# Graph kernel: tables and first projection in one stage, with keys and values projected under the tables

## The reference

```
q = (x @ Wq + bq).reshape(n, H, C)
k = (x @ Wk + bk).reshape(n, H, C)
v = (x @ Wv + bv).reshape(n, H, C)
e = (ea @ We).reshape(-1, H, C)
kj = k[src] + e
vj = v[src] + e
alpha = einsum('ehc,ehc->eh', q[dst], kj) / sqrt(C)
...
return out + x @ Ws + bs
```

## Time and profile before

| what | us |
|---|---|
| runs | 8291.74, 8230.95, 8294.77 |
| median | 8291.74 |
| profiled execution | 8250.71 |
| its span | 8248.9 |
| busy: PE, PEld, DVE | 3484.3, 2716.4, 3757.1 |
| busy: ACT, POOL | 2123.0, 3625.4 |

### The profile page before, as it was taken

How to read it: one execution, slowest core, us unless ns; L and a number is a source line. 1 busy time by engine, 2 the same in 40 slices (tenths; PEclk the granted TensorE clock), 3 DMA queues, 4 the chain that set the end, 5 groups by cost and what they waited for, 6 DMA issues and landing times. The chain is left out here.

```text
span 8248.9 us, 101168 instructions
## 1 busy us (share of the span) xinstructions
PE 3484.3 (42%) x20097; PEld 2716.4 (33%) x20099; DVE 3757.1 (46%) x8522; ACT 2123.0 (26%) x5629; POOL 3625.4 (44%) x3965
## 2 busy tenths in 40 slices
PE   3445544545444444444355457324233334333332
PEld 1344444444233334334232223112222223222322
DVE  5444444445644444444664347796233333223333
ACT  1333333333144434334322224255000001000001
POOL 1444443443154444443026650022666664566664
PEclk8676767677756656556666669656555566655556
DMA  3333333333332222222111111001111112111111
GB/s 115 118 104 104 109 108 103 109 107 101 106 92 83 81 84 81 81 80 75 48 51 32 32 36 58 18 0 67 43 44 44 44 45 77 57 44 45 45 44 49
DMA packets 371112, 569.20 MB, mean 69 GB/s; under 512 B 86858, under 2 KB 247772, under 8 KB 370524
## 3 DMA queue, kind: packets, MB, share of 16 engines
q0 software_dynamic: 140272, 311.94, 13.8%
q1 hardware_dynamic: 230764, 256.45, 9.4%
HBM read 509.24 MB, written 58.86 MB: 69 GB/s over the span
## 5 line engine op out<-in xcount | busy, mean ns | idle before, releaser
L682 POOL DMA_INDIRECT ring<-kv_table,idx x1568 | 1494.9, 953 | 1950.7 <-ACT pv L771 1268.1
L2017 POOL DMA_INDIRECT rows_in<-rel_table,idx x1568 | 1489.4, 950 | 808.3 <-issue 610.3
L1196 PE MATMUL ps_s<-rows_in,onehot 128*128 x3520 | 741.0, 393 | 1622.0 <-SPq L2033 850.6
L1196 PEld LDWEIGHTS ps_s<-rows_in,onehot 128*128 128x128 f32 x3520 | 683.0, 296 | 1680.0 <-issue 1679.0
L891 DVE TENSOR_TENSOR key<-ps_q,key 128x528 f32<-128x528 f32 x440 | 306.8, 707 | 1524.2 <-remote 1070.6
L1223 DVE TENSOR_TENSOR acc<-acc,ps_s 128x128 f32 x880 | 253.0, 288 | 1478.8 <-PE ps_s L1196 1065.2
L815 PE MATMUL ps_s<-pv,lent 128*128 128x136 f32 x3520 | 819.4, 386 | 106.6 <-DVE acc L874 94.9
L829 PE MATMUL ps_q<-qsplit,st 128*128 x5280 | 503.7, 255 | 739.9 <-DVE key L891 348.8
L815 PEld LDWEIGHTS ps_s<-pv,lent 128*128 128x128 f32 x3520 | 704.0, 279 | 145.7 <-DVE acc L874 118.1
L829 PEld LDWEIGHTS ps_q<-qsplit,st 128*128 128x128 bf16 x5280 | 413.3, 113 | 826.9 <-issue 801.3
L1726 PE MATMUL ps_f<-s_split,at_lo 128*128 128x392 bf16 x2112 | 510.6, 402 | 357.1 <-DVE found L1783 248.5
(11 more groups left out here) (322 smaller groups left out, 5058.1 us busy)
## 6 DMA issues: line engine op xcount, KB each, us to landing
dl_row<-dloc_slots SPq DMA_DIRECT2D x132, 640.0 KB
eb<-in_edge_attr SPq DMA_DIRECT2D x440, 128.0 KB
ring<-kv_table,idx POOLq DMA_INDIRECT x1568
rows_in<-rel_table,idx POOLq DMA_INDIRECT x1568
flags<-flag_rows SPq DMA_DIRECT2D x88, 168.0 KB
rel_table<-y_out SPq DMA_DIRECT2D x14, 1024.0 KB, 4.3
lo_row<-lo_rows SPq DMA_DIRECT2D x44, 256.0 KB
rel_table<-y_out SPq DMA_DIRECT2D x14, 768.0 KB, 3.6
```

Of the source, the lines that this page charges most:

```text
L682: pool.indirect_dma_start(ring3[:, s % (2 * RING), :], None, kv_table, bass.IndirectOffsetOnAxis(ap=idx[:, s:s + 1], axis=0))\
L1196: last_mm = pe.matmul(to, one(n, j), ring_rows(places[m], j), start=(j == 0), stop=(j == 1))
L2017: pool.indirect_dma_start(rows3[:, t, :], None, table, bass.IndirectOffsetOnAxis(ap=idx[:, t:t + 1], axis=0))\
```

## The change

`opening` takes the place of `tables` and of the first `conv_project`; there is one barrier less. The loads of x, weights and biases (ten) are issued behind the twelve of the tables.

Keys and values of all seven groups are made in a first loop. It begins when VectorE has copied the tile rows out of PSUM, for the loop uses that PSUM as its four places. ScalarE copies x to `xg` and the transposed x to `xt`, and takes the results out; PE multiplies a window with 256 columns and adds the bias by a second matmul of one row (`ones` by the bias row). SP stores them in a loop that stands ahead of the table stores on its queue. PE's loop stands ahead of the transposes of the extremes and of the three tables, ScalarE's ahead of its three copies.

Skips and queries are made in a second loop behind the turned tables: x is transposed a second time, GpSimd copies to `xg`, PE multiplies 256 columns per window, VectorE adds the biases, makes the parts in the same chain of seven, and ScalarE copies them to `qsplit`. SP stores the skips behind the table stores. The matmul that spreads the extremes (`ext_d`) stands behind PE's second loop, and VectorE's last operations on them behind its own.

```diff
-        def tables():
-            done = ExitStack()
+        def opening(x_in, qsplit):
...
+                ps_y = pb(done, "ps_y", [P, 2 * 1024])
+                ps_x = pb(done, "ps_x", [P, 1024])
                 ps_t = pb(done, "ps_t", [P, 512])
-                ps_e = pb(done, "ps_e", [P, 2 * 1024])
+                ps_row, ps_e = ps_y, ps_y
...
+                PLACES, N_LOADS, Q_LINKS = 4, 10, 7
+                kv3, sq3, qx3 = grouped(kv_out), grouped(sq_out), grouped(qx)
+                q3 = qsplit[:, :].rearrange("p (w k c) -> p w k c", k=3, c=QW)
+                place_in = lambda j: ps_y[:, j % PLACES * 512:j % PLACES * 512 + 2 * D]
...
+                        sp.dma_start(x_in[:, :], a["x"]).then_inc(project_in.sem, 16)
+                        for n, k in enumerate(("v", "k", "s", "q")):
+                            sp.dma_start(w_all[:, n * D:(n + 1) * D], a[f"L0_gnn_W{k}1"]).then_inc(project_in.sem, 16)
+                            sp.dma_start(b_all[:, n * D:(n + 1) * D],
+                                         a[f"L0_gnn_b{k}1"].partition_broadcast(P)).then_inc(project_in.sem, 16)
+                        sp.dma_start(we_b[:, :], a["L0_gnn_We1"][0, :].partition_broadcast(P)).then_inc(project_in.sem, 16)
+
+                        with sp.Fori(0, NG) as g:
+                            for (lo, hi), sig in zip(HALVES, kv_stored):
+                                sp.wait_ge(evacuated.sem, evacuated.at(g * G + hi))
+                                sp.sem_inc(issuing.sem, 1)
+                                sp.dma_start(kv_rows[:, bass.ds(g * G + lo, hi - lo), :], kv3[:, lo:hi, :]).then_inc(sig.sem, 16)
 
                         sp.wait_ge(chained.sem, LAYOUT_T)
...
                         sp.wait_ge(copied.sem, len(to_turn))
                         sp.dma_start(type_rows[0], et16_e[:, :]).then_inc(stored.sem, 16)
+
+                        with sp.Fori(0, NG) as g:
+                            for (lo, hi), sig in zip(HALVES, skip_stored):
+                                sp.wait_ge(added.sem, added.at(g * G + hi))
+                                sp.sem_inc(issuing.sem, 1)
+                                sp.dma_start(skip_of[:, bass.ds(g * G + lo, hi - lo), :], sq3[:, lo:hi, 0:D]).then_inc(sig.sem, 16)
                         sp.wait_ge(stored.sem, 16 * STORES)
+                        sp.dma_start(last_of, last_row[:, 0:SP // 2]).then_inc(last_in.sem, 16)
+                        for sig in kv_stored + skip_stored:
+                            sp.wait_ge(sig.sem, sig.at(16 * NG))
+                        sp.wait_ge(last_in.sem, 16)
...
                         dve.wait_ge(chained.sem, link.count[0])
+                        dve.sem_inc(of_rows.sem, 1)
...
+                        dve.wait_ge(project_in.sem, 16 * N_LOADS)
+                        with dve.Fori(0, NG) as g:
+                            for j in range(G):
+                                if j in starts:
+                                    sig = skip_stored[starts.index(j)]
+                                    dve.wait_ge(sig.sem, sig.at(g * 16))
+                                dve.wait_ge(made.sem, made.at(g * G + (NW + j + 1)))
+                                dve.tensor_tensor(sq3[:, j, :], place_in(j), b_all[:, 2 * D:4 * D], ALU.add).then_inc(added.sem, 1)
+                            dve.wait_ge(added.sem, added.at((g + 1) * G))
+                            dve.wait_ge(kept.sem, kept.at(g))
+                            q_link = chain(dve, q_chain, g * Q_LINKS)
+                            q_link(dve.tensor_scalar(qx3[:, :, 0:D], sq3[:, :, D:2 * D], float(C) ** -0.5, None, ALU.mult))
+                            q_link(dve.tensor_tensor(grouped(tmp), qx3[:, :, 0:D], we_b[:, :].unsqueeze(1).to_broadcast([P, G, D]), ALU.mult))
+                            q_link(dve.tensor_reduce(qx3[:, :, D:QW], tmp[:, :].rearrange("p (g h c) -> p g h c", g=G, h=H), AX.X, ALU.add))
+                            split3(dve, q_link, qx, rest, parts)
+                            assert q_link.count[0] == Q_LINKS
+                            dve.sem_inc(results.sem, 1)
...
+                        def half_of(g, first, biased):
+                            pe.wait_ge(got.sem, got.at(g + (1 if biased else NG + 1)))
+                            pe.wait_ge(xt_ready.sem, xt_ready.at(g + (0 if biased else NG)))
+                            for j in range(G):
+                                last_mm = pe.transpose(ps_x[:, j * D:(j + 1) * D], xg[:, j * D:(j + 1) * D], ident[:, :])
+                            last_mm.then_inc(x_turned.sem, 1)
+                            pe.wait_ge(xt_ready.sem, xt_ready.at(g + (1 if biased else NG + 1)))
+                            used_up = evacuated if biased else added
+                            for j in range(G):
+                                pe.wait_ge(used_up.sem, used_up.at(g * G + max(j - PLACES + 1, 0)))
+                                last_mm = pe.matmul(place_in(j), xt[:, j * D:(j + 1) * D], w_all[:, first:first + 2 * D],
+                                                    start=True, stop=not biased)
+                                if biased:
+                                    last_mm = pe.matmul(place_in(j), ones[0:1, 0:P], b_all[0:1, first:first + 2 * D],
+                                                        start=False, stop=True)
+                                last_mm.then_inc(made.sem, 1)
+
+                        pe.wait_ge(of_rows.sem, 1)
+                        pe.wait_ge(project_in.sem, 16 * N_LOADS)
+                        with pe.Fori(0, NG) as g:
+                            half_of(g, 0, True)
+
                         pe.wait_ge(chained.sem, LAYOUT_T)
                         pe.transpose(ps_t[0:2, 128:256], ext[:, :], ident[:, :]).then_inc(ext_s.sem, 1)
-                        pe.wait_ge(counted.sem, TC + 1)
-                        pe.matmul(ps_t[:, 256:258], ones[0:2, :], ext_d[:, :], start=True, stop=True).then_inc(ext_s.sem, 1)
+                        pe.wait_ge(evacuated.sem, evacuated.at(NW))
                         for n, (of, _) in enumerate(to_turn):
                             if n >= 2:
                                 pe.wait_ge(copied.sem, n - 1)
@@ -360,13 +457,56 @@
                                 last_mm = pe.transpose(ps_e[:, at:at + P], blocked(of)[:, b, :], ident[:, :])
                             last_mm.then_inc(turned.sem, 1)
 
+                        pe.wait_ge(copied.sem, len(to_turn))
+                        with pe.Fori(0, NG) as g:
+                            half_of(g, 2 * D, False)
+                        pe.wait_ge(counted.sem, TC + 1)
+                        pe.matmul(ps_t[:, 256:258], ones[0:2, :], ext_d[:, :], start=True, stop=True).then_inc(ext_s.sem, 1)
...
+                        def take(g, before):
+                            act_e.wait_ge(x_turned.sem, x_turned.at(g + (before // G + 1)))
+                            act_e.wait_ge(made.sem, made.at(g * G + before))
+                            act_e.copy(xt[:, :], ps_x[:, 0:G * D]).then_inc(xt_ready.sem, 1)
+
+                        def store_results(g):
+                            act_e.wait_ge(results.sem, results.at(g + 1))
+                            act_e.copy(q3[:, bass.ds(g * G, G), :, :],
+                                       parts[:, :].rearrange("p (k g c) -> p g k c", k=3, g=G)).then_inc(kept.sem, 1)
+
+                        def fetch_x(g):
+                            act_e.copy(xg[:, :], x_in[:, bass.ds(g * (G * D), G * D)]).then_inc(got.sem, 1)
+
+                        def keep_kv(g):
+                            for j in range(G):
+                                if j in starts:
+                                    sig = kv_stored[starts.index(j)]
+                                    act_e.wait_ge(sig.sem, sig.at(g * 16))
+                                act_e.wait_ge(made.sem, made.at(g * G + j + 1))
+                                act_e.copy(kv3[:, j, :], place_in(j)).then_inc(evacuated.sem, 1)
+
+                        act_e.wait_ge(project_in.sem, 16 * N_LOADS)
+                        act_e.wait_ge(of_rows.sem, 1)
+                        fetch_x(0)
+                        with act_e.Fori(0, NG - 1) as g:
+                            take(g, 0)
+                            fetch_x(g + 1)
+                            keep_kv(g)
+                        take(NG - 1, 0)
+                        keep_kv(NG - 1)
+
                         for n, (_, to) in enumerate(to_turn):
                             act_e.wait_ge(turned.sem, n + 2)
                             at = n % 2 * 1024
                             act_e.copy(to[:, :].rearrange("e (p b) -> e b p", b=SB),
                                        ps_e[:, at:at + SP].rearrange("e (b p) -> e b p", b=SB)).then_inc(copied.sem, 1)
+
+                        take(0, NW)
+                        with act_e.Fori(1, NG) as g:
+                            take(g, NW)
```

(57 more changed lines are left out.)

5 lines of the change are left out of this document (2 added, 3 removed).

## The result

| | before | changed |
|---|---|---|
| median, us (21 runs each) | 8281.87 | 8305.44 |
| lowest to highest | 8230.95 to 8312.67 | 8268.81 to 8339.28 |
| profiled span | 8248.9 | 8337.5 |
| end of the opening in it | 219.8 | 259.3 |

The changed kernel is **slower**: ratio 1.0037, 95% interval 1.0021 to 1.0053, which is 31 us (17 to 44). The opening alone is 39.5 us longer, inside that interval. (The two profiled executions lie 88.6 us apart, but single executions of one kernel differ by some 80 us; the stretch of relation scores alone took 58 us longer in this one, and nothing was changed in it. In runs 1 to 4, where nothing was changed in it either, it took between 965 and 995 us, against 976 and 1034 in these two. So the prediction's sign that a stage behind the opening moves by over 10 us did appear, but a single pair of profiles can't carry it.)

The account below looks back on a forecast made before the run. The opening, 219.8 of 8248.9 us, was read as five successive stretches with most engines idle. Overlapped, its steps summed to 186.5, 33 us less; against the mean 8272.5 that gave 8240 us, range 8195 to 8286.

Parts of the forecast that it names:

- a stage behind the opening moves by over 10 us: Sign of being wrong: stages behind the opening change their length by more than 10 us.
- (2) keys and values: First loop, under VectorE's tables: seven groups of 8.3 us, the first starting cold, 63.4 us in all, ending at 93.1.
- (3) turned tables: Behind the first loop: first transpose to last copy as before, 6.8 us, entered as 6.9, ending at 100.0.
- (4) to the first matmul: Start of skips and queries: cold transposes and copy, 2.8 us, first matmul at 102.8.
- chain, hop and stall: First group of skips and queries: VectorE's chain, hop and 1 us waiting for the first skip store, 8.7 us together.
- six groups, chain of the last: Remaining skips and queries: six groups of 11.2 us from 117.2, 66.6 us, ending at 183.8.
- rival A: Keys and values stay at the low clock: groups of 14.9 us, opening 9 us slower than before, 8281 us; chance 0.10.
- Rival B: One-row matmul in keys and values nearly free: their phase ends at 71, 52 us less in all; chance 0.08.
- C: Gathers and kv stores hinder each other, so VectorE's tables end behind 93; a 37 us wait leaves 23 less; chance 0.07.
- D: Skips and queries at full clock without stall: 7 and 1 us better, 41 less; edge of the sum, no separate chance.
- E: No overlap because PE's program order puts keys and values behind the tables; the prediction denied it, no chance given.
- Step (1): Start: nine more semaphores, about 0.5 us; new loads cost 0, bound +3; loop released at 29.7 us.

Follow-up runs that it names:

- run 1: Changed kernel with the bias matmul over 128 rows (1/128 each) instead of one: ratio to before 0.9939, opening ends at 186.43 us.
- run 2: Changed kernel without the bias matmul of keys and values, so their biases are missing from the result: opening ends at 167.9 us.
- run 3: Changed kernel with the bias matmul over 64 rows instead of one: 1.15 us a matmul, clock 0.50, first table store at 167.1 us.
- Run 4: Changed kernel with the one-row bias matmuls issued in batches of four and three ahead of the real ones: opening ends at 218.2 us.
- run 5: Changed kernel with one row in all matmuls of the keys and values loop: 0.853 us a matmul, loop ends at 140 us.
- run 6: Changed kernel with the bias matmul over 96 rows instead of one: opening ends at 186.9 us.
- run 10: 128-row float32 bias version with SP issuing the ten new loads only after the twelve table loads: opening ends at 187.3 us.
- run 8: Kernel before with only a one-row bias matmul added per window of its first projection: 8080.62 us against 7994.46, stage ends at 342.
- run 7: Changed kernel with the bias as three bfloat16 parts in a 128-row matmul: ratio to before 0.9943, opening ends at 172.3 us.
- run 9: Changed kernel with 64 rows in both matmuls of the keys and values loop: 0.853 us a matmul, loop ends near 139 us.
- run 12: Changed kernel with the float32 bias over 128 rows, timed again on another chip: 6918.70 us against 6952.5 before, ratio 0.9952.

## Why the prediction was wrong, point by point

The forecast was 8240 us (8195 to 8286) and no change by more than 1%; it is 8305, slower by 0.4%. That is under 1%, but the opening was to become 33 us shorter and became 39.5 longer. The sum had one wrong step:

| step of the sum | forecast us | measured us |
|---|---|---|
| release of the loop | 29.7 | 30.9 |
| (2) keys and values | 63.4 | 135.3 |
| (3) turned tables | 6.9 | 7.2 |
| (4) to the first matmul | 2.8 | 3.1 |
| first windows | 5.7 | 5.2 |
| chain, hop and stall | 8.7 | 9.6 |
| six groups, chain of the last | 66.6 | 65.4 |
| last copy | 2.7 | 2.6 |
| end | 186.5 | 259.3 |

Behind step (2) the forecast was 93.4 us and the measurement 93.1. Two more lines of the changed kernel show one group of skips and queries, 10.8 us; the five from 191.35 on are 11.1 on average (10.4 to 11.8), against the 11.2 of the sum:

```profile
202.49 1.84 DVE L395 TENSOR_TENSOR sq_out<-ps_y,b_all 128x256 f32<-128x256 f32 x5 [0.64 <-DVE parts L654]
...
213.29 1.42 DVE L395 TENSOR_TENSOR sq_out<-ps_y,b_all 128x256 f32<-128x256 f32 x4 [0.63 <-DVE parts L654]
```

**Step (2) failed.** The sentence was: "All rows here go by columns (448, 512 and 640), so I take the full price." Each of those lines has 128 rows of stationary operand. They show that the price goes by columns where all 128 rows are used, and I carried it over to an operand of one row, alternating with full ones. The 71.9 us that it was short are, in the parts that the runs give:

- 41.5 us, what the other two leave: seven groups at the 1.2 GHz level (14.9 us a group without changes). This is rival A, priced at 42 us and given 0.10; run 5 has it with one change a group left (15.1 us).
- 29.1 us: 98 changes of kind, 14 a group, at 0.297 us. No step and no rival had this. Run 4 measures it, and run 1 removes it together with the low clock.
- 1.3 us: ScalarE's table load, moved from the start of the program to just behind the release.

The evidence that I set against rival A was a later projection that stayed at 1.00 across its gaps. That spoke about gaps, and A was about rows. For rows I had no line at all, and the honest reading of "no row of before tells" would have been an even chance, not one in ten.

I weighed the wrong rule. The Trainium skill, TensorE: Matmul & The Clock Gate, section Why this matters for your kernels, says that a single matmul of 32 rows takes the time of one of 128. Of a matmul by itself that holds here for one row too: 0.853 us at the low level (run 5), as for 128 in run 1's first group. The Trainium skill, TensorEngine Tiling (Array Packing), section Tiling Modes, says under its key properties that a change of tiling mode drains TensorE, and it lists row tilings of 128, 64 and 32 rows. Runs 1, 3, 4 and 6 agree: 96 rows go with 128 at no cost, 64 and one beside 128 cost 0.29 us a change. That the halt falls between these sizes, at this price, and that the next weight load then doesn't run ahead, was shown; that a switch of tiling mode is behind it is argued from the Trainium skill. By that rule the sum would have had 98 changes at an unknown price, and the bound of "nothing" would have been seen to be on the wrong side.

**Rival B** (one-row matmul nearly free) did not happen. **C** did not either: the wait for the gathers was 8.9 us against 8.1 with kv stores beside them (8.4 in run 1, where the stores come at the forecast pace), and VectorE's tables ended at 76.2. **D** did not either: it needs groups of 10.1 us and no stall, and they were 11.1 at a granted clock of 0.76, with a stall of 2.5 us (3.9 in run 1). **E** is ruled out by the trace of the change itself: the loop's first matmul runs at 33.14.

**Step (1)** was right in size: the loop was released 1.2 us late, within the bound of 3 us. Whether the new loads did that is not shown (run 10).

**The range.** It reached to A, and A was one of the two costs, so the time fell outside by 19 us. With an unmeasured operand in 49 matmuls, the upper end should have lain above A, for instance by that matmul's price once more: 49 x 0.853 = 42 us over A's 8281, an estimate that would have reached 8323.

## What to carry to other kernels

Before an instruction gets its price, compare it with the row in every size, not only in the one that is thought to set the time; a matmul whose stationary operand has few rows is another case, to be measured by itself. Adding a bias, or anything small, by a short matmul among full ones cost a halt at each change here and left TensorE at its low clock; fill the operand to all 128 rows with a share of the value, in bfloat16 parts where float32 would be two records. Work that is moved under a cover is worth what it costs there, and if it outlasts its cover, all that was queued behind it on each engine and on SP is late by the difference.

## What the runs showed of the hardware that was not expected

- A change between a matmul of 128 rows and one of 64 rows or one cost 0.29 us at the 1.2 GHz level, in both directions (runs 3, 4, 8), and 0.19 us between one and 128 at the 2.4 GHz level (run 4). Between 96 and 128 rows, and between float32 and bfloat16, nothing was lost (runs 6, 7).
- TensorE stayed at 1.2 GHz for over 100 us with matmuls of one row (run 5) or 64 rows (run 9, clock 0.50) that followed each other without a halt, and with 64 or one row in every second matmul (run 3, the changed kernel). With 96 or 128 rows it rose within the first group (runs 1, 6, 7). The same one-row matmuls in batches of four and three let it rise and fall (run 4), so how they are ordered matters as well as the rows. Why was not shown.
- The clock column of a stretch read 1.00 where no change of level had been recorded yet. Run 5 and run 9 have the same 0.853 us a matmul and read 1.00 and 0.50 from 52 to 70 us; go by the spacing of records.
- The kernel before took 8310, 7994, 6926 and 6952 us on four chips, with nothing changed. The one kernel profiled on two of them (runs 1 and 12) opened in 186.4 and 183.2 us; its first sum over edges took 3668 us on the first and 2672 on the other. Why was not looked into.
